# A graph-attention start-up put in a new order: exponentials shifted by an early maximum, a bound for the scale, three PSUM sets, and copies of Wh by ScalarE alone

## The chip, the cores and the metric

One NeuronCore of one Trainium2 chip runs the whole program. The metric is device time in microseconds. The engines are TensorE (PE, with its weight loads PEld), VectorE (DVE), ScalarE (ACT), GpSimd (POOL) and SyncE (SP); each runs its own instructions in the order in which the kernel writes them and waits for the others through semaphores.

## The reference, cut to what matters

```
Wh = x @ W                                       # x is 8192 x 128, W is 128 x 128
e  = leaky_relu((Wh @ a1)[:, None] + (Wh @ a2)[None, :], 0.2)   # s_i + t_j
e  = where(adj > 0, e, -9e15)                    # adj is 8192 x 8192 int32, sparse
x  = layernorm(x + elu(softmax(e, axis=1) @ Wh))
x1 = (adj @ x) / deg
x  = layernorm(x + concat([x1, x]) @ weight + bias)
```

## The kernel before

With s = Wh @ a1 and t = Wh @ a2, the exponential of leaky_relu(s_i + t_j) is a product of a factor of row i and a factor of column j, with one pair of factors where s_i + t_j is positive and another pair where it is negative. So the kernel makes, for each of the 64 tiles of 128 columns j, `factors`: Wh times e_j = exp(t_j - c) and Wh times f_j = exp(0.2 (t_j - c)), each as a high and a low float16 part, scaled by `scale_e` = 2^14 / max|Wh|, plus a denominator column for each part and a column of ones. The shift c is the largest t of all 8192. The main work of the first layer is then a matmul of 0/1 masks (edges that are positive, edges that are negative) with these factors (L679). Rows go in 32 groups of 256; a group takes 64 column tiles in eight `h` of 8 tiles, and an `h` is 4 x 8 matmuls (two row tiles times positive and negative). PE also packs the adjacency bits into 16-bit words (`pack_bits`, L640, for the first pair of groups, `pack_tile` in between matmuls, L628, later), ACT copies the words out of PSUM (`copy_words`, L422), and makes the level masks (`first_scores` L436 for the first group, `scores` L466 later). DVE unpacks words (L936, L938) and splits them into negative and positive masks (L1013, L1020). The second layer (L758, L819) follows after about 1000 us; the change does not touch it.

The change touches only the start, up to the end of the first group. There, in this order:

- SP loads x in nine pieces into the space of `factors[:, 1]`. PE turns W and makes W @ a (L594, L597), then for 16 blocks k of four tiles turns x (`turn_x`, L608) and multiplies by W and W @ a (`make_wh`, L617). A block goes to one of two pairs of PSUM banks. For each block ACT copies the turned x (`copy_turned`, L416), DVE copies s and t out of PSUM (`copy_s_t`, L865, semaphore wh_ok), and then ACT copies Wh out (`copy_wh`, L428, which waits for wh_ok). DVE also takes the largest |Wh| of each block (L871).
- After the last block DVE takes the largest and the smallest t, POOL makes them largest over the partitions (L366), ACT takes the exponentials e and f of all 64 tiles at once (L457, L458), and POOL reduces the largest |Wh| (L368).
- POOL issues the adjacency loads (L358), four of the first pair of groups after the sixth x piece, then those of the second pair, one after each `pack_bits`. Two `pack_bits` stand ahead of the first matmuls on PE.
- Then for each quarter c of the columns (16 tiles) DVE multiplies Wh by e and by f (`make_product` L923), ACT makes the high parts (`high_of` L504), and DVE the low parts (`low_of` L1028, `low_half` L1037 in the last quarter), unpacks and splits masks, and PE multiplies.

A product space has three slots. Each engine's order is written out by hand, so one engine that waits holds back all that stands behind it on that engine. What a group 1 matmul needs first is its masks (two ScalarE scores of 8 tiles for a quarter, an unpack, two splits) and the sums of group 0 taken off PSUM (L1051).

Of the kernel before, what the change touches and what calls it, by code (L numbers as in the profile page):

```python
# [32 lines left out]
P = 128  # L33
# [17 lines left out]
WIDEST = 10.0  # L51
# [7 lines left out]
def adj_resnorm_kernel(nc, x, adj, w0, a0, w1, b1, consts, out):  # L59
# [21 lines left out]
    with ctx:  # L81
# [3 lines left out]
        def sem(name):  # L85
# [11 lines left out]
        cols = sb("cols", [P, 12, NJ], F32)  # L97
# [9 lines left out]
        wh_top = sb("wh_top", [P, NX], F32)  # L107
# [6 lines left out]
        s_col, t_col, t_big, e_col, f_col, u_col, v_col, y_col, uy_col, vy_col, e_den, f_den = \  # L114
            (cols[:, k, :] for k in range(12))
        t_max, _, wh_max, wh_one, neg_t, neg_ft, inv_wh, scale_e, ones, sum_x = (one[:, k:k + 1] for k in range(10))
        t_max, t_spread = top_low[:, 2:3], wide_one[:, 7:8]
# [9 lines left out]
        wh = words[:, NG // 2:, :].rearrange("p g w -> p (g w)").bitcast(F32)[:, 0:NJ * F]\  # L127
            .rearrange("p (j f) -> p j f", f=F)
        early = words[:, 2:NG // 2, :].rearrange("p g w -> p (g w)").bitcast(F32)
        sizes, at, early_of = dict(product=3 * UNIT * F, wq=F + 2, w_turn=P, a_sb=2,  # L130
# [4 lines left out]
        product = early_of["product"].rearrange("p (k j f) -> p k j f", k=3, f=F)  # L135
        x_in = factors[:, 1, :, :].rearrange("p j r -> p (j r)").bitcast(F32)[:, 0:NJ * F]\
            .rearrange("p (k j f) -> p k j f", k=NX, f=F)
        x_t = product[:, 2, 0:2 * XB, :].rearrange("p (k j) f -> p k (j f)", k=2)
# [18 lines left out]
        pack_ps = [ctx.enter_context(nc.psum_tensor(f"pack_ps{k}", [P, 512], F32)) for k in range(2)]  # L157
# [16 lines left out]
        x_turned, x_t_ok, wh_made, wh_ok, top_ok = (sem(n) for n in "x_turned x_t_ok wh_made wh_ok top_ok".split())  # L174
        s_turned, s_turn_ok, sum_x_ok, sum_xb_ok = (sem(n) for n in "s_turned s_turn_ok sum_x_ok sum_xb_ok".split())
        mean_made, mean_ok, one_row_ok = (sem(n) for n in "mean_made mean_ok one_row_ok".split())
        t_top_ok, t_max_ok, wh_one_ok, wh_max_ok = (sem(n) for n in "t_top_ok t_max_ok wh_one_ok wh_max_ok".split())
        neg_ok, y_ok_col, uy_ok, exp_cols_ok, t_big_ok = (sem(n) for n in "neg_ok y_col_ok uy_ok exp_cols_ok t_big_ok".split())
        guard_ok, inv_ok, scale_ok, den_ok, den_hi_ok = (sem(n) for n in "guard_ok inv_ok scale_ok den_ok den_hi_ok".split())
# [55 lines left out]
        def wh_banks(k):  # L235
            return acc_banks[:, 2 * (k % 2):2 * (k % 2) + 2, 0:2 * (F + 2)].rearrange("p h (j f) -> p h j f", j=2)
# [115 lines left out]
        def _(pool):  # L352
# [7 lines left out]
            pool.memset(minus_half, -0.5).then_inc(half_ok, 1)  # L360
            pool.wait_ge(x_in_sem[NX // 2 - 3], 16)
            for c in range(UPG):
                load_adj(0, c, first=True)
            pool.wait_ge(t_top_ok, 1)
            pool.wait_ge(low_ok, 2)
            pool.partition_all_reduce(top_low[:, 2:4], top_low[:, 0:2], P, bass.bass_isa.ReduceOp.max).then_inc(t_max_ok, 1)  # L366
            pool.wait_ge(wh_one_ok, 1)
            pool.partition_all_reduce(wh_max, wh_one, P, bass.bass_isa.ReduceOp.max).then_inc(wh_max_ok, 1)  # L368

# [32 lines left out]
        def _(act):  # L402
# [3 lines left out]
            act.wait_ge(w0_turned, 1)  # L406
            act.activation(w_turn, turn_ps[0][:, 0:P], ACT.Copy).then_inc(w_turn_ok, 1)
            act.wait_ge(wa_made, 1)
            act.activation(wq[:, F:F + 2], turn_ps[1][:, 0:2], ACT.Copy).then_inc(wa_ok, 1)

# [14 lines left out]
            def copy_wh(k):  # L425

                act.wait_ge(wh_ok, k + 1)
                act.activation(wh[:, XB * k:XB * (k + 1), :].rearrange("p (h j) f -> p h j f", h=2),  # L428
                               wh_banks(k)[:, :, :, 0:F], ACT.Copy).then_inc(wh_copied, 1)
# [11 lines left out]
            for k in range(NX):  # L441
# [5 lines left out]
                if k:  # L447
                    copy_wh(k - 1)
            copy_wh(NX - 1)
            act.wait_ge(s_row_ok, 1)  # L450
            act.wait_ge(s_turned, 1)
            act.activation(s_turn, turn_ps[0][:, 0:P], ACT.Copy).then_inc(s_turn_ok, 1)
            first_scores(0, 2)


            act.wait_ge(neg_ok, 2)
# [24 lines left out]
            def group(g, slot, loads, next_words, before_last=None, second=False):  # L481
# [3 lines left out]
                for h in range(8):  # L485
                    if h or not second:
                        scores(g, slot, h)
                    if second and h == UPG + 1:
                        act.wait_ge(wh_saved, 1)
                        act.wait_ge(e_low_ok, UPG + 1)  # L490
                        act.wait_ge(f_low_ok, UPG + 1)
# [863 lines left out]
```

## Time and profile before

| | |
|---|---|
| median of three runs | 1486.92 us (1486.07 to 1487.76) |
| profiled execution, its span | 1484.3 us |
| what lies around the span | about 2.6 us (median less span) |
| PE busy in the span | 1449.9 us (98%) |
| DVE, ACT, POOL busy | 994.9, 936.4, 118.3 us |
| granted TensorE clock, mean | 0.991 |

The span runs from the first to the last instruction of one profiled execution. "Idle before" in a row of the timeline is the time in which the engine had nothing to do just ahead of that row, and the arrow says what ended it. In timeline rows several instructions of one kind are merged: the count stands behind the x and the length is that of all together. An instruction's length overlaps the start of the next one by about 0.1 us on DVE and ACT, so the text reckons from start to start.

### The profile page before, as it was taken

To read this page: it belongs to the slowest core of one execution; us is meant where nothing else is said; L and a number is where in the kernel's file an instruction comes from. 1 tells how busy PE (TensorE), PEld (TensorE's weight loads), DVE (VectorE), ACT (ScalarE), POOL (GpSimd) and SP (SyncE) were. 2 spreads that over 40 slices of the span, in tenths; PEclk is the share of its full clock that TensorE was granted. 3 is DMA by queue.
4 is the path that set the end of the run, shared out by engine and by line. 5 is a ranking of instruction groups with operands and counts; after the bars stand their busy time and mean duration, and the time that the engine had idled before them with its cause. 6 is when DMAs were issued, how large, how long until landed. Compare 5 with 4: busy or idle time off the path is not lost.

```text
span 1484.3 us, 33988 instructions
## 1 busy us (share of the span) xinstructions
PE 1449.9 (98%) x12110; PEld 1107.8 (75%) x12110; DVE 994.9 (67%) x2833; ACT 936.4 (63%) x2289; POOL 118.3 (8%) x199
## 2 busy tenths in 40 slices
PE   7599999999999999999999999999999999999998
PEld 7578888888888888888888888884454545454557
DVE  4998888888788888878887887773433343334332
ACT  6989999999999999999999999940000000000000
POOL 1001000100010010001000100000000000000000
PEclk9799999999999999999999999999999999999999
DMA  9969997788788868877886882041000000000000
GB/s 174 111 71 101 120 108 90 83 94 95 84 86 96 93 78 95 94 90 82 95 94 83 87 96 37 19 119 49 22 15 21 14 21 14 21 14 21 14 15 15
DMA packets 99201, 101.47 MB, mean 68 GB/s; under 512 B 4432, under 2 KB 66384, under 8 KB 99152
## 3 DMA queue, kind: packets, MB, share of 16 engines
q0 software_dynamic: 33792, 67.11, 45.5%
q1 hardware_dynamic: 64800, 33.57, 8.7%
q8 instruction: 31, 0.51, 0.1%
q10 hardware_dynamic: 560, 0.14, 0.1%
q14 instruction: 18, 0.15, 0.0%
HBM read 289.48 MB, written 12.65 MB: 204 GB/s over the span
## 4 chain that ended last, share of the span: by engine, by line
PE 90%; DMA 2%; DVE 1%; issue 0%; POOL 0%; ACT 0%; SPq 0%; DVEq 0%; POOLq 0%
PE acc L679 58%; PE pack_ps L758 27%; PE pack_ps L819 2%; DMA adj_space<-in_adj 2%; PE acc L793 1%; PE pack_ps L628 1%; PE turn_ps L780 1%; PE turn_ps L769 0%; DMA level_ring<-x_rows 0%; DMA x_parts<-parts 0%; POOL one L378 0%; DVE adj_space L945 0%; DVE stats L1118 0%; DVE part_sums L1051 0%; DVE edge_ring L1020 0%
## 5 line engine op out<-in xcount | busy, mean ns | idle before, releaser
L466 ACT ACTIVATE level_ring<-s_row,cols 128x256 fp8e4<-128x256 f32 x1984 | 803.7, 495 | 0.0
L679 PE MATMUL acc<-factors,edge_ring 128*128 128x259 f16 x4096 | 548.8, 274 | 14.5 <-DVE edge_ring L1020 13.0
L679 PE MATMUL acc<-factors,level_ring 128*128 128x259 f16 x4096 | 548.3, 274 | 0.0
L758 PE MATMUL pack_ps<-adj_space,factors 128*128 128x512 fp8e4 x1920 | 421.7, 379 | 0.9 <-issue 0.9
L679 PEld LDWEIGHTS acc<-factors,edge_ring 128*128 128x128 fp8e4 x4096 | 365.9, 98 | 64.8 <-issue 15.8
L679 PEld LDWEIGHTS acc<-factors,level_ring 128*128 128x128 fp8e4 x4096 | 366.5, 98 | 48.9
L758 PEld LDWEIGHTS pack_ps<-adj_space,factors 128*128 128x128 f16 x1920 | 187.9, 98 | 217.6 <-issue 1.1
L1013 DVE TENSOR_TENSOR level_ring<-level_ring,edge_ring 128x1024 uint16<-128x1024 uint16 x256 | 171.2, 689 | 103.7 <-ACT level_ring L466 93.3
L1190 DVE TENSOR_SCALAR adj_space<-words 128x512 uint16 (+1 forms) x448 | 96.3, 288 | 146.7 <-PE pack_ps L758 146.6
L628 PE MATMUL pack_ps<-pack_w,adj_space 128*128 128x32 bf16 x960 | 170.7, 178 | 0.0
L1020 DVE TENSOR_TENSOR edge_ring<-edge_ring,level_ring 128x1024 uint16<-128x1024 uint16 x256 | 166.7, 683 | 0.1
L558 ACT ACTIVATE level_ring<-turn_ps 128x512 f32<-128x512 f32 x16 | 9.6, 597 | 217.4 <-PE turn_ps L769 217.4
L566 ACT ACTIVATE level_ring<-pack_ps 128x256 f32<-128x256 f32 x30 | 9.9, 381 | 212.6 <-PE pack_ps L758 212.6
L936 DVE TENSOR_SCALAR edge_ring<-words 128x512 uint16 (+1 forms) x448 | 106.1, 297 | 8.6 <-issue 6.4
L376 POOL TENSOR_SCALAR one<-mv 128x2 f32<-128x2 f32 x64 | 18.9, 295 | 1075.1 <-DVE mv L1125 1075.1
L628 PEld LDWEIGHTS pack_ps<-pack_w,adj_space 128*128 128x128 fp8e4 x960 | 91.6, 95 | 14.1
L1219 DVE SCALAR_TENSOR_TENSOR level_ring<-acc,cols,level_ring 128x128 f32<-128x128 f32 x64 | 19.4, 346 | 96.8 <-PE acc L793 96.8
L945 DVE SCALAR_TENSOR_TENSOR adj_space<-adj_space 128x1024 int32<-128x1024 int32 x60 | 73.1, 1218 | 0.9 <-DMA adj_space<-in_adj 0.9
L358 POOL DMA_DIRECT2D adj_space<-in_adj x64 | 51.3, 802 | 260.5 <-PE pack_ps L628 195.8
L422 ACT ACTIVATE words<-pack_ps 128x512 f32 (+1 forms) x64 | 38.1, 595 | 39.7 <-PE pack_ps L628 39.7
L378 POOL TENSOR_TENSOR one<-one 128x2 f32<-128x2 f32 x64 | 48.0, 750 | 9.5
L1130 DVE TENSOR_SCALAR level_ring<-level_ring,mv,one 128x128 f32<-128x128 f32 x64 | 19.3, 344 | 41.5 <-POOL one L378 41.5
(104 smaller groups left out, 726.8 us busy)
## 6 DMA issues: line engine op xcount, KB each, us to landing
adj_space<-in_adj POOLq DMA_DIRECT2D x64, 1024.0 KB, 14.5
rows_x<-in_x SPq DMA_DIRECT2D x32, 128.0 KB, 2.1
x_rows<-rows_y SPq DMA_DIRECT2D x32, 128.0 KB, 9.7
x_parts<-parts SPq DMA_DIRECT2D x32, 128.0 KB, 4.4
factors<-x_parts SPq DMA_DIRECT2D x8, 512.0 KB, 4.8
level_ring<-x_rows SPq DMA_DIRECT2D x16, 256.0 KB, 2.8
out<-level_ring SPq DMA_DIRECT2D x32, 128.0 KB, 1.8
s_row<-s_and_t SPq DMA_DIRECT2D x30, 128.0 KB, 3.0
```

The lines of the kernel that those rows point to most:

```text
L358: pool.dma_start(adj_ring[:, c, :, :], adj_tiles[n, :, :, c * COLS:(c + 1) * COLS]).then_inc(adj_in[c], 16)
L378: pool.tensor_tensor(rstd, var_eps, minus_half, ALU.pow).then_inc(rstd_sem, TPG)
L422: act.activation(row_words[:, n, c * WPU:(c + 1) * WPU], pack_ps[c % 2][:, 0:WPU], ACT.Copy)\
L466: a = act.activation(level_bytes[:, h % MASK_SLOTS, j, :], s_row[:, slot, :], ACT.Relu, bias=t_big[:, h * HALF + j:h * HALF + j + 1], scal ...
L628: return pe.matmul(pack_ps[c % 2][:, j * WPR:(j + 1) * WPR], nibbles, pack_w[:, 0, :], start=True, stop=True)
L679: m = pe.matmul(acc[a][:, 0:WIDE_ROW], mask, factors[:, neg, jj, 0:WIDE_ROW], start=(jj == 0), stop=(jj == NJ - 1))
L758: m = pe.matmul(pack_ps[slot][:, :], factors[:, 0, jj, part * F:(part + 1) * F], ring_1_bytes[:, c, j, :], start=(jj == 0 and part == 0), ...
L936: d = dve.tensor_scalar(to, src, 6 - k, EDGES, ALU.logical_shift_left, ALU.bitwise_and)
L945: dve.scalar_tensor_tensor(out=pair[:, 0], in0=pair[:, 1], scalar=1, in1=pair[:, 0], op0=ALU.logical_shift_left, op1=ALU.bitwise_or).then_ ...
L1013: dve.tensor_tensor(level, level, edge_ring[:, c % EDGE_SLOTS, k * HALF:(k + 1) * HALF, :], ALU.bitwise_and).then_inc(neg_ready, 1)
L1020: dve.tensor_tensor(edges, edges, level_ring[:, (2 * c + k) % MASK_SLOTS, :, :], ALU.bitwise_xor)\
L1190: d = dve.tensor_scalar(to, src, 6 - k, EDGES, ALU.logical_shift_left, ALU.bitwise_and)
```

## The change

- `base`, the largest t of the first 16 tiles (over all partitions), replaces the largest t of all as shift c. `t_exp` is t bounded from above by base + 1. e and f are made in four quarters (`exponentials(c)`) and no longer at once. The test for a wide spread of t is adapted (`WIDEST` 7.5, `RISE` 1).
- `wh_one`, from which the scale comes, is no longer the largest |Wh| but the product of the largest |x| (`top_of_x`, nine reductions) and the largest absolute column sum of W.
- ACT copies Wh and the two columns s and t in one instruction (`copy_wh`, now 130 columns a tile), and DVE's copies (L865) and maxima (L871) go. The s column of that space is then overwritten with `wh_one`, so product, high part and low part have 129 columns and make the denominators too; the six DVE instructions for denominators (L956, L962, L971) go.
- `make_wh` uses three PSUM sets (two of `acc`, one of `pack_ps`). W is turned after x's first block.
- Inside the loop of 16 blocks ACT now also makes 8 `first_scores` (k = 6 to 13), two quarters of exponentials (k = 8, 11) and `high_of(0)` (k = 14).
- POOL takes `base` over the partitions ahead of the adjacency loads, and takes over y, uy and vy from DVE.
- PE does `pack_bits(0)` and `(1)`, then turns s and t, and goes to the masks' matmuls. DVE and ACT have a new order by hand in the first group.

```diff
-            for k in range(NX):
+            copy_turned(0)
+            act.wait_ge(w0_turned, 1)
+            act.activation(w_turn, pack_ps[0][:, 0:P], ACT.Copy).then_inc(w_turn_ok, 1)
+            copy_turned(1)
+            act.wait_ge(wa_made, 1)
+            act.activation(wq[:, F:F + 2], pack_ps[0][:, P:P + 2], ACT.Copy).then_inc(wa_ok, 1)
+            copy_wh(0)
+            for k in range(2, NX):
                 copy_turned(k)
...
-                if k:
-                    copy_wh(k - 1)
+                copy_wh(k - 1)
+                if 6 <= k < 14:
+                    first_scores(k - 6, k - 5)
+                if k == 8:
+                    exponentials(0)
+                if k == 11:
+                    exponentials(1)
+                if k == 14:
+                    high_of(0)
             copy_wh(NX - 1)
...
+            exponentials(2)
+            high_of(1)
+            first_scores(8, 12)
+            copy_words(0, 0)
+            exponentials(3)
+            first_scores(12, 16)
+            high_of(2)
+            first_scores(16, 20)
+            copy_words(0, 1)
             act.wait_ge(s_turned, 1)
             act.activation(s_turn, turn_ps[0][:, 0:P], ACT.Copy).then_inc(s_turn_ok, 1)
...
+            high_of(3)
+            first_scores(20, 32)
+            high_of(4)
+            high_of(5)
+            first_scores(32, 40)
+            copy_words(0, 2)
+            first_scores(40, 48)
+            high_of(6)
+            high_of(7)
+            copy_words(0, 3)
+            first_scores(48, 64)
+            act.wait_ge(uy_ok, 2)
+            act.activation(u_col, uy_col, ACT.Exp).then_inc(exp_cols_ok, 1)
+            act.activation(v_col, vy_col, ACT.Exp).then_inc(exp_cols_ok, 1)
...
+            def first_unpack(c):
+                dve.wait_ge(mask_used, 2 * c + 2)
+                dve.wait_ge(words_ok, c + 1)
+                unpack(0, 0, c, edge_ring, c).then_inc(unpacked, 1)
+            def split(c, k):
+                negative(0, c, k)
+                positive(0, c, k)
...
+            top_column(0)
+            make_product(0)
+            scaled_t(2)
+            bounded_t(2)
+            top_column(1)
+            make_product(1)
+            low_of(0, e_low_ok)
+            dve.wait_ge(wh_copied, NX)
...
+            top_column(2)
+            top_column(3)
+            make_product(2)
+            first_unpack(0)
+            split(0, 0)
+            dve.wait_ge(x_turned, NX)
+            dve.memset(factors[:, 1, :, ROW:WIDE_ROW], 1.0).then_inc(edge_col_ok, 1)
+            low_of(1, f_low_ok)
+            split(0, 1)
+            make_product(3)
+            low_of(2, e_low_ok)
...
+            first_unpack(1)
+            split(1, 0)
+            low_of(3, f_low_ok)
+            split(1, 1)
+            make_product(4)
+            make_product(5)
+            low_of(4, e_low_ok)
+            first_unpack(2)
+            split(2, 0)
+            low_of(5, f_low_ok)
+            split(2, 1)
+            make_product(6)
+            make_product(7)
+            sum_of_x()
+            low_of(6, e_low_ok)
+            first_unpack(3)
+            low_of(7, f_low_ok)
+            split(3, 0)
+            split(3, 1)
```

## Rows read from the trace of the kernel before

**Rows 1.** The page, part 4: lines on the chain that ended last.

```profile
PE acc L679 58%; PE pack_ps L758 27%; PE pack_ps L819 2%; DMA adj_space<-in_adj 2%; PE acc L793 1%; PE pack_ps L628 1%; PE turn_ps L780 1%; PE turn_ps L769 0%; DMA level_ring<-x_rows 0%; DMA x_parts<-parts 0%; POOL one L378 0%; DVE adj_space L945 0%; DVE stats L1118 0%; DVE part_sums L1051 0%; DVE edge_ring L1020 0%
```

**Rows 2.** Busy time by stretch: PE, PEld, DVE, ACT, POOL, PEclk, DMA share, GB/s.

```profile
40.00:50.00 10.00, 1.89 (x44) 1.49 (x39) 9.81 (x23) 10.00 (x20) 0.74 (x1) 0.50 1.07 115
200.00:400.00 200.00, 200.00 (x1975) 176.44 (x1974) 164.09 (x424) 188.33 (x468) 19.43 (x28) 1.00 0.81 92
```

**Rows 3.** Timeline of PE: start us, length us, line, work, count, idle before.

```profile
7.14 0.56 PE L597 MATMUL turn_ps<-words 128*128 128x2 f32 x2 [1.62 <-DMA words<-in_a]
...
9.85 2.10 PE L617 MATMUL acc<-words 128*128 128x130 f32 x8
...
21.00 0.60 PE L608 MATMUL turn_ps<-consts_sb,factors 128*128 128x128 f32 x4
21.43 1.06 PE L617 MATMUL acc<-words 128*128 128x130 f32 x8
...
39.23 1.87 PE L640 MATMUL pack_ps<-pack_w,adj_space 128*128 128x32 bf16 x64 [3.92 <-issue]
...
50.12 1.89 PE L679 MATMUL acc<-factors,edge_ring 128*128 128x259 f16 x8 [7.28 <-DVE edge_ring L1020]
...
93.21 1.05 PE L679 MATMUL acc<-factors,edge_ring 128*128 128x259 f16 x8 [0.54 <-DVE part_sums L1051]
```

**Rows 4.** Timeline of ACT, the same columns.

```profile
16.80 0.19 ACT L416 ACTIVATION_READ_ACCUMULATOR words<-turn_ps 128x1 f32 x1
16.89 0.59 ACT L445 ACTIVATE s_row<-pack_ps 128x512 f32<-128x512 f32 x1
...
33.36 0.60 ACT L428 ACTIVATE words<-acc 128x512 f32<-128x512 f32 x1 [0.70 <-DVE cols L865]
...
35.19 0.35 ACT L457 ACTIVATE cols<-cols,one 128x64 f32<-128x64 f32 x1 [0.27 <-DVE one L897]
...
38.87 0.58 ACT L422 ACTIVATE words<-pack_ps 128x512 uint16<-128x512 f32 x1
39.35 3.89 ACT L504 ACTIVATE factors<-words,one 128x2048 f16<-128x2048 f32 x2
...
43.61 8.09 ACT L436 ACTIVATE level_ring<-s_row,cols 128x256 fp8e4<-128x256 f32 x20
```

**Rows 5.** Timeline of DVE, the same columns.

```profile
34.95 0.14 DVE L896 TENSOR_SCALAR one<-top_low 128x1 f32<-128x1 f32 x1
...
47.05 0.90 DVE L936 TENSOR_SCALAR edge_ring<-words 128x512 uint16<-128x512 uint16 x4
...
50.39 4.49 DVE L923 TENSOR_TENSOR words<-words,cols 128x2048 f32<-128x2048 f32 x2
54.80 4.61 DVE L1028 SCALAR_TENSOR_TENSOR factors<-words,one,factors 128x2048 f16<-128x2048 f32 x2
...
83.68 0.68 DVE L1013 TENSOR_TENSOR level_ring<-level_ring,edge_ring 128x1024 uint16<-128x1024 uint16 x1
84.40 0.69 DVE L1020 TENSOR_TENSOR edge_ring<-edge_ring,level_ring 128x1024 uint16<-128x1024 uint16 x1
```

**Rows 6.** Timeline of POOL, the same columns.

```profile
14.43 3.18 POOL L358 DMA_DIRECT2D adj_space<-in_adj  x4 [13.46 <-DMA factors<-in_x]
34.01 0.38 POOL L366 PARTITION_ALL_REDUCE top_low<-top_low  x1 [16.40 <-DVE top_low L890]
...
71.71 0.74 POOL L358 DMA_DIRECT2D adj_space<-in_adj  x1 [9.81 <-PE pack_ps L640]
```

**Rows 7.** Issue to landing of the adjacency load issued at 14.43 us.

```profile
DMA to landing us min/median/max: 14.3/14.3/14.3
```

**Rows 8.** Issue to landing of the adjacency load issued at 71.71 us.

```profile
DMA to landing us min/median/max: 26.8/26.8/26.8
```

**Rows 9.** Issue to landing of the adjacency load issued at 115.73 us.

```profile
DMA to landing us min/median/max: 13.0/13.0/13.0
```

**Rows 10.** Issue to landing of the second x load, issued at 1.39 us.

```profile
factors<-in_x SPq DMA_DIRECT2D x1, 512.0 KB, 5.4
```

More of the change, by code:

```diff
@@ L113, in adj_resnorm_kernel @@
         ident = consts_sb[:, 0:P]
[L114 to L117, printed above, removed]
+        s_col, t_col, t_big, e_col, f_col, u_col, v_col, y_col, uy_col, vy_col, t_exp = \
+            (cols[:, k, :] for k in range(11))
+        x_most, w_most, _, wh_one, neg_t, neg_ft, inv_wh, scale_e, ones, sum_x = (one[:, k:k + 1] for k in range(10))
+        x_most, w_most = tops[:, 2:3], tops[:, 3:4]
+        base_top, base, base_rise = tops[:, 4:5], tops[:, 5:6], tops[:, 6:7]
+        t_max, t_spread, t_rise = top_low[:, 2:3], wide_one[:, 7:8], tops[:, 7:8]
         half_max, row_max, neg_max, half_sum, row_sum = (wide_one[:, a:b] for a, b in ((0, 2), (2, 3), (3, 4), (4, 6), (6, 7)))
@@ L613, in make_wh @@
                 pe.wait_ge(x_t_ok, k + 1)
-                if k >= 2:
-                    pe.wait_ge(wh_copied, k - 1)
+                if k == 6:
+                    pe.wait_ge(s_row_ok, 1)
+                elif set_of[k] in set_of[0:k]:
+                    last = max(i for i in range(k) if set_of[i] == set_of[k])
+                    pe.wait_ge(wh_copied, last + 1)
                 for j in range(XB):
@@ L652, in _ @@
             turn_x(0)
+            pe.wait_ge(w0_in, 16)
+            pe.transpose(pack_ps[0][:, 0:P], wq[:, 0:F], ident).then_inc(w0_turned, 1)
+            turn_x(1)
+            pe.wait_ge(w_turn_ok, 1)
+            pe.wait_ge(a0_in, 16)
+            pe.matmul(pack_ps[0][:, P:P + 2], w_turn, a_sb, start=True, stop=True).then_inc(wa_made, 1)
+            pe.wait_ge(wa_ok, 1)
             for k in range(NX):
-                if k + 1 < NX:
+                if 0 < k < NX - 1:
                     turn_x(k + 1)
@@ L696, in group @@
                         multiply(g, h, pack_chunk=pack_chunk)
-            pe.wait_ge(wh_copied, NX)
-            pack_bits(1)
-            wide = is_wide(pe)
-            pe.wait_ge(sum_xb_ok, 1)
-            pe.matmul(turn_ps[1][:, 0:F], sum_xb, wq[:, 0:F], start=True, stop=True).then_inc(mean_made, 1)
-            pe.wait_ge(den_hi_ok, 4)
-            pe.wait_ge(edge_col_ok, 1)
             for c in range(UPG):
                 for h in (2 * c, 2 * c + 1):
-                    multiply(0, h, c == UPG - 1 or h % 2 == 0, True)
+                    multiply(0, h, h % 2 == 0, True)
                 if c < 2:
                     pack_bits(c + 2)
+                if c == 1:
+                    wide = is_wide(pe)
+                if c == 2:
+                    pe.wait_ge(sum_xb_ok, 1)
+                    pe.matmul(turn_ps[1][:, 0:F], sum_xb, wq[:, 0:F], start=True, stop=True).then_inc(mean_made, 1)
             group(1, {1: (1, 0), 2: (1, 1), 3: (1, 2)})
```

298 lines of the change are left out of this document (135 added, 163 removed).

## The prediction

> **What bounds the kernel now.** I read the chain that ended last first: PE's own matmuls hold it [rows 1]. The table of stretches then shows where PE is not full: from 200 us on it is busy all the time at full clock, and in the start it is busy 1.89 of 10 us between 40 and 50 us, at half clock, while VectorE and ScalarE are full [rows 2]. So the end moves by as much as the first matmul of group 1 moves (93.21 us [rows 3]), if nothing later catches up or falls behind. ScalarE is busy 188.33 of 200 us in the steady part [rows 2], so what is late there comes back slowly, and PE, which is the bound, never gives it back. Last I read the timelines of the start for each operation's price.
>
> **Prices, start to start.** ScalarE: a copy of 512 columns 0.49 us, the accumulator read 0.09, words 0.48, a high part 1.90 (two in 3.89), a score 0.40 (20 in 8.09), an exponential of 64 columns 0.25 and of 16, by estimate, 0.15 [rows 4]. VectorE: product 2.20 (two in 4.49), low part 2.27, unpack until its first use 0.95, negative and positive mask of one h 0.72 and 0.61, so a `split` 1.33, small ones 0.08 [rows 5]. A full 129-column product, high or low part is 0.01 longer. PE: `turn_x` 0.43, `make_wh` 0.90; cold, `make_wh` 1.9 [rows 3]. A semaphore adds about 0.05, an estimate from the gap between a length's end and the next engine's start. With the order of the kernel before, these prices and waits put group 1 at 93.0, against 93.21 measured, so they carry a sum over engines.
>
> **The head.** The second x load lands at 1.39 + 5.4 = 6.8 [rows 10]. W @ a now stands behind `turn_x(1)`, not ahead of both turns; with cold turns it ends near 8.3, `make_wh(0)` starts near 8.9 and not at 9.85 [rows 3]. That 0.95 is mostly lost again in the first blocks, which alternate PE and ScalarE: I reach the accumulator read of block 4 at 16.7 (16.80 before [rows 4]).
>
> **The loop.** What is removed, VectorE's copy between `make_wh` and `copy_wh` and its reductions of Wh, is a wait that hardly counted: PE's 0.43 + 0.90 = 1.33 us a block [rows 3] was the pace, and ScalarE's 0.49 + 0.09 + 0.49 = 1.07 fitted in. The third PSUM set removes a wait behind which PE was full anyway. What is added counts: with one score a block ScalarE needs 1.48, and becomes the pace. After the read at 16.7 ScalarE has 0.09, s_row 0.52, copy_wh(3) 0.50, eleven blocks of 1.08 (11.9), 8 scores (3.2), 4 exponentials (0.6), high_of(0) (1.9) and the last copy (0.5), in all 19.2, and waits 1.1, of which 0.8 for `make_wh(15)`, which high_of(0) has held back. So it leaves the loop at 37.0; before it did at 33.36 + 0.49 = 33.85 [rows 4]. The loop ends **3.1 us later**, with 8 scores (3.2), all but two of the exponentials and one high part (1.9) done ahead.
>
> VectorE's nine reductions of x (1.1 each by the product's rate of 2048 elements in 2.2) follow the loads, and lie beside the loop. The scale is ready near 26.8, the first product at 29.5, three us before high_of(0) at 32.7 wants it. POOL's reduction over partitions isn't longer than 0.94: 34.01 to the consumer's 34.95, which shows no wait [rows 5, 6]; up to 3 us more would stay covered there.
>
> **Adjacency.** The loads now wait for `base`, so they are issued at 19.0 and not at 14.43 [rows 6]. A lone load lands after 13.0 [rows 9]; queued ones follow each 10 us (the first landed 14.3 after its issue at 14.43, at 28.7, and the eighth at 71.71 + 26.8 = 98.5 [rows 6 to 8]: (98.5 - 28.7) / 7). New landings: 32.0, 41.9, 51.8, 61.8, then to 101.5. `pack_bits(1)` can't start before 41.95 (39.23 before [rows 3]), and now stands ahead of every masks' matmul: the first matmul is at 43.9 instead of 50.12 [rows 3]. Words of the second quarter are used only at 52, so these 2.7 us are covered. Joins of the second pair move later with group 1 and keep 15 us of margin.
>
> **After the loop**, the likeliest course, link by link:
> - ScalarE from 37.0: two exponentials, high(1), four scores, words(0): 4.4. VectorE, idle 1.0, unpacks at 41.4.
> - VectorE: unpack 0.95, split, low(1), split, product(3), low(2), 0.4 of small ones, unpack 1.25 (0.3 of it a wait for a score), split, low(3), split, product(4) 2.35: 19.2. ScalarE is done with scores 20 to 31 at 56.4 and **waits 4.2** for product(4), after 2.4 for product(3). It gets it at 60.65.
> - ScalarE: high(4), 0.3 wait, high(5), eight scores, words(2): 8.0. VectorE **waits 3.6** for words(2), until 68.6; the score that the next split wants comes no earlier.
> - VectorE: unpack, split, low(5), split, product(6): 8.2, to 76.8. ScalarE **waits 5.2**.
> - ScalarE: high(6), 0.3, high(7), words(3), 16 scores (6.4), u and v (0.3), 16 scores of group 1 (6.4): 17.8, to 94.6. VectorE waits 1.9, 1.1 and 2.6 for scores.
> - VectorE: mask operations 1.8, the scaling of group 0's sums 0.55: 2.4. Group 1 starts at **97.1**.
>
> 37.0 + 4.4 + 19.2 + 8.0 + 8.2 + 17.8 + 2.4 = 97.0. The work of both engines alone would have allowed less: the two of them hand over in turn, with 11.8 us of ScalarE waiting for products. PE starts 6.2 us earlier than before and loses it in waits of 0.7, 5.9 and 4.7 for masks; the cold clock that follows them falls in time it does not need. What VectorE is spared (denominators, about 1.5, and y, uy and vy, 0.3) is on no wait of this chain.
>
> Against the profile (my 93.0 for 93.21) this is +4.1 us: span 1488.4, median 1486.92 + 4.1 = **1491.0**.
>
> **A rule of the Trainium skill.** The POOL rows show no lock: four load issues took 3.18 us beside VectorE's work, 0.8 each [rows 6]. "SBUF — State Buffer", section "SBUF: two separate sides", says that GpSimd and VectorE share a port pair as an exclusive lock, and that a DMA issued by GpSimd can starve for its descriptors. By it, POOL's loads, and y, uy and vy which it now computes, could be late beside VectorE's two-input products; the trace can't show the lock itself.
>
> **Rivals.**
> - *The waits overlap, faster.* If VectorE gets to product(4) 4 us earlier than I sum, ScalarE does not stop, and the later waits shrink. Bound: VectorE's own list from 37.2 (six products 13.3, seven low parts 16.0, four unpacks 3.8, eight splits 10.6, group 1's masks and sums 4.0, rest 2.2) ends at 87.1, so group 1 at 87.1, -6.1 us: 1480.8. It decides from 4 us less waiting on. For it: both engines have the work done ahead. Against: each handover is in the written order. 12%.
> - *The loop costs less, no change.* A clock that rises at 10 us and waits of 0.03 for 0.05 give group 1 near 95.3, +2.3: 1489.2. 24%, with all that ends within 0.2%.
> - *As summed, or up to 2 us more.* Cold turns until 15 us give 98.4, +5.4. 52%.
> - *Adjacency late, by the port or the queue.* Landings 6 us later put group 1 at 97.9 and from there each us costs one; 9 us give +8: 1495. By the rule above this is where it would show. 12%.
> - *The exact path.* If the test for wide t fired, 64 slow tiles would follow. From the reference's inputs the largest t is 1.46, the first 16 tiles' 1.14, the smallest -1.49: both tests are under 7.5. 0%.
>
> **Numbers.** Changes of 0.2% (3.0 us) are about what a measurement of this kernel can tell. Slower by more: 0.62 (most of the summed case and the late adjacency). Within: 0.25. Faster: 0.13. The likeliest case's own range is 1489.2 to 1493.0. The range takes in the cheap loop and the late adjacency, and a part of an overlap: 1485.0 to 1495.0.
>
> **What would show it.** Right: ScalarE's last `copy_wh` at 36 to 37; first masks' matmul at 43 to 45; ScalarE idle some 4 us ahead of the fifth high part and 5 ahead of the seventh; VectorE idle 3 to 4 ahead of the third unpack; group 1 at 96 to 98.5; later stages shifted by the same amount. Wrong: no idle at these handovers, or PE waiting for `pack_bits(1)` past 45, or a later stage which moves by another amount than group 1.

## The result, and the profile after

The changed kernel takes **1490.70 us** (median of 14 runs, 1489.70 to 1491.41) against 1487.24 us (14 runs, 1486.07 to 1488.27) for the kernel before: ratio 1.0022, 95% interval [1.0015, 1.0029]. That is slower by 3.5 us; the forecast was 1491.0, slower by 4.1. In the profiled executions the span went from 1484.3 to 1488.8 us, by 4.5, at the same mean TensorE clock (0.991 and 0.992). The profiled execution of the changed kernel took 1490.74 us, as its median, 1.9 more than its span. Where the kernel before has its time and its span on record for the same execution (58 of them, beside the experiments), the time is 1.7 to 1.8 us longer, and not the 2.6 that the table ahead of the prediction has by setting a median against the span of another execution. By estimate, then, the profiled execution of before took 1486.05 us, 1.2 below its median. That makes the 4.5 us of the spans and the 3.5 of the medians one finding.

The table of stretches for the kernel before, from the end of the loop to the start of group 1 (columns: stretch, its length, busy us of PE, PEld, DVE, ACT, POOL with their counts, granted clock, DMA share, GB/s):

```profile
37.00:99.00 62.00, 45.22 (x503) 37.76 (x504) 60.44 (x91) 61.08 (x124) 2.23 (x3) 0.81 1.04 109
```

The same stretch, and the steady one of [rows 2], for the changed kernel:

```profile
37.00:99.00 62.00, 42.69 (x518) 34.82 (x515) 51.70 (x76) 49.74 (x100) 7.43 (x8) 0.83 1.06 111
200.00:400.00 200.00, 200.00 (x1975) 176.43 (x1972) 162.52 (x415) 188.45 (x467) 19.14 (x28) 1.00 0.82 92
```

Read these first. In the start both VectorE and ScalarE had been full (60.44 and 61.08 of 62 us); now each is idle for 10 to 12 us of it, and still group 1 starts later. That is not less work. A fixed stretch counts only what falls into it: VectorE now does 3.9 us more ahead of 37 us (19.77 for 15.90) and ScalarE 1.5 (25.66 for 24.14), and what waits pushed behind 99 us is not counted. Up to its first matmul of group 1 each kernel keeps VectorE busy for the same time, 70.72 us before and 70.73 now. ScalarE has 79.43 and 74.65, but before it had made 36 scores of group 1 by then and now 23, which is about those 5 us. VectorE's copies and maxima (L865 and L871, 13.5 us) are gone, but nine reductions of x (9.8 us) and other small ones came in their place. What the change brought is work done earlier and idle time behind it. From 200 us on PE is full as it was in [rows 2], so what the start loses stays lost.

The timeline of PE, changed kernel (columns as in [rows 3]):

```profile
8.54 2.10 PE L648 MATMUL acc<-words,edge_ring 128*128 128x130 f32 x8 [0.35 <-ACT words L477]
...
13.88 1.21 PE L648 MATMUL acc<-words,edge_ring 128*128 128x130 f32 x8
...
42.24 1.89 PE L671 MATMUL pack_ps<-pack_w,adj_space 128*128 128x32 bf16 x64 [3.75 <-DMA adj_space<-in_adj]
...
44.67 1.89 PE L720 MATMUL acc<-factors,edge_ring 128*128 128x259 f16 x8 [0.25 <-DVE factors L1195]
...
72.31 1.89 PE L720 MATMUL acc<-factors,edge_ring 128*128 128x259 f16 x8 [6.13 <-DVE edge_ring L1001]
...
87.61 1.89 PE L720 MATMUL acc<-factors,edge_ring 128*128 128x259 f16 x8 [6.01 <-DVE edge_ring L1001]
...
98.26 1.05 PE L720 MATMUL acc<-factors,edge_ring 128*128 128x259 f16 x8 [0.93 <-DVE part_sums L1023]
```

The masks' matmuls start 5.45 us earlier than in [rows 3] (44.67 for 50.12), and group 1 starts 5.05 us later (98.26 for 93.21). Between the two, PE stands idle for 6.1 us ahead of the third quarter's masks and for 6.0 ahead of the fourth's. A stage later 0.4 of the 5.05 came back: group 2's first matmul is at 158.09 with 0.51 us of idle ahead of it, where before it was at 153.41 with 0.88; the rest of the span moved as group 2 did, within 0.2 us.

The timeline of ACT, changed kernel:

```profile
36.94 0.60 ACT L441 ACTIVATE words<-acc 128x520 f32<-128x520 f32 x1 [0.76 <-PE acc L648]
...
50.38 2.04 ACT L469 ACTIVATE factors<-words,one 128x2064 f16<-128x2064 f32 x1 [2.31 <-DVE words L938]
...
61.66 2.04 ACT L469 ACTIVATE factors<-words,one 128x2064 f16<-128x2064 f32 x1 [4.46 <-DVE words L938]
...
77.88 2.03 ACT L469 ACTIVATE factors<-words,one 128x2064 f16<-128x2064 f32 x1 [5.12 <-DVE words L938]
```

The timeline of DVE, changed kernel:

```profile
42.02 0.90 DVE L951 TENSOR_SCALAR edge_ring<-words 128x512 uint16<-128x512 uint16 x4 [0.89 <-ACT words L435]
...
69.67 0.90 DVE L951 TENSOR_SCALAR edge_ring<-words 128x512 uint16<-128x512 uint16 x4 [3.55 <-ACT words L435]
...
89.08 0.69 DVE L994 TENSOR_TENSOR level_ring<-level_ring,edge_ring 128x1024 uint16<-128x1024 uint16 x1 [1.77 <-ACT level_ring L449]
...
92.56 0.69 DVE L994 TENSOR_TENSOR level_ring<-level_ring,edge_ring 128x1024 uint16<-128x1024 uint16 x1 [0.81 <-ACT level_ring L527]
...
95.75 0.69 DVE L994 TENSOR_TENSOR level_ring<-level_ring,edge_ring 128x1024 uint16<-128x1024 uint16 x1 [2.50 <-ACT level_ring L527]
```

ScalarE waits for VectorE's products (L938) at 50, 62 and 78 us, VectorE waits for ScalarE's words (L435) at 42 and 70 and for scores from 89 on. Each wait ends when the other engine has come out of its own. The chain that ended last between 38 and 98 us shows the same in order, with start and length of each piece (pieces under 0.1 us are left out):

```profile
59.32 4.53 DVE words L938 x2
63.87 2.03 ACT factors L469
65.91 2.02 ACT level_ring L449 x6
67.93 0.26 issue
68.19 0.89 ACT level_ring L449 x2
69.08 0.49 ACT words L435
69.67 0.16 DVE edge_ring L951
...
75.54 4.53 DVE words L938 x2
80.09 2.04 ACT factors L469
82.13 0.47 ACT words L435
82.60 2.43 ACT level_ring L449 x7
```

After 42 us it crosses between the two engines four times, and among the pieces that the view lists none is of PE, POOL or a DMA.

### The profile page after: what moved, and what is told of

Its sections match the earlier page's. It is cut to its first block, busy times and chain, and to the rows that moved or that the text cites. A ratio compares the mean times of both kernels' runs of the same rounds, so it can differ in the third digit from the quotient of the medians.

```text
span 1488.8 us, 34001 instructions
## 1 busy us (share of the span) xinstructions
PE 1453.4 (98%) x12110; PEld 1109.4 (75%) x12110; DVE 994.3 (67%) x2816; ACT 937.0 (63%) x2295; POOL 121.0 (8%) x203
## 4 chain that ended last, share of the span: by engine, by line
PE 92%; ACT 3%; DMA 2%; DVE 2%; issue 1%; POOL 0%; DVEq 0%; SPq 0%; POOLq 0%; ACTq 0%
PE acc L720 58%; PE pack_ps L797 28%; PE pack_ps L858 2%; DMA adj_space<-in_adj 2%; PE acc L832 1%; PE pack_ps L659 1%; PE turn_ps L819 1%; ACT level_ring L449 1%; DVE words L938 1%; PE acc L648 1%; PE turn_ps L808 0%; ACT factors L469 0%; ACT level_ring L527 0%; DMA factors<-in_x 0%; DVE factors L1009 0%
## 5 line engine op out<-in xcount | busy, mean ns | idle before, releaser
L720 PE MATMUL acc<-factors,edge_ring 128*128 128x259 f16 x4096 | 549.6, 275 | 14.4 <-DVE edge_ring L1001 12.7
L435 ACT ACTIVATE words<-pack_ps 128x512 f32 (+1 forms) x64 | 38.0, 594 | 39.3 <-PE pack_ps L659 39.3
L1102 DVE TENSOR_SCALAR level_ring<-level_ring,mv,one 128x128 f32<-128x128 f32 x64 | 19.3, 344 | 41.5 <-POOL one L396 41.5
```

The costliest lines, as they stand in the source:

```text
L435: act.activation(row_words[:, n, c * WPU:(c + 1) * WPU], pack_ps[c % 2][:, 0:WPU], ACT.Copy)\
L720: m = pe.matmul(acc[a][:, 0:WIDE_ROW], mask, factors[:, neg, jj, 0:WIDE_ROW], start=(jj == 0), stop=(jj == NJ - 1))
```

## The experiments

Each ran beside the kernel before on the same chip; that kernel's medians there were 1487.32, 1487.37 and 1487.23 us. Diffs are against the changed kernel unless said otherwise. "Group 1" is the start of its first matmul, 98.26 us in the changed kernel. Of 12 kernels I begin with those that undo one part each.

**1. Two PSUM sets.**

```diff
-        set_of = [0, 1, 0, 1, 0, 1, 2, 0, 1, 2, 0, 1, 2, 0, 1, 0]
+        set_of = [k % 2 for k in range(NX)]
```

> The changed kernel with two PSUM sets in place of three. If the third set buys nothing (the copies of Wh and of turned x on ScalarE are the pace of the loop, and PE is full before that): group 1 starts at 98.3 as in the changed kernel, within 0.3, time 1490.7 within 1. If the third set hides a wait in the loop, the loop of 16 blocks gets up to 0.4 us longer in each of the ten blocks from k = 6 on, up to 4 us in all: 1491.5 to 1494.7.

Measured: 1490.86 us, 1.0021 [1.0012, 1.0031]. The loop ended with a copy at 36.93 (36.94) and group 1 began at 98.28. The third set is worth nothing: PE's queue is never held by a set in this loop.

**2. The adjacency loads later**, behind POOL's second reduction.

```diff
             pool.partition_all_reduce(base, base_top, P, bass.bass_isa.ReduceOp.max).then_inc(base_ok, 1)
+            pool.wait_ge(x_top_ok, NX // 2 + 3)
+            pool.partition_all_reduce(tops[:, 2:4], tops[:, 0:2], P, bass.bass_isa.ReduceOp.max).then_inc(x_w_ok, 1)
             pool.wait_ge(x_in_sem[NX // 2 - 3], 16)
...
-            pool.wait_ge(x_top_ok, NX // 2 + 3)
-            pool.partition_all_reduce(tops[:, 2:4], tops[:, 0:2], P, bass.bass_isa.ReduceOp.max).then_inc(x_w_ok, 1)
```

> The changed kernel with the first four adjacency loads behind POOL's second reduction, issued at 26.4 and not at 18.96. Handover theory: pack_bits(1) and the first masks' matmul come 7 us later (near 49.5 and 52), of which the wait for product(3) and VectorE's list behind it swallow 5: group 1 at 100.4, +2.2, time 1492.9. Adjacency theory: all 7 us go through, 1497.7.

Measured: 1492.68 us, 1.0038 [1.0023, 1.0052]; issue at 25.40 for 18.96. The timeline of PE with the late loads:

```profile
49.31 1.89 PE L671 MATMUL pack_ps<-pack_w,adj_space 128*128 128x32 bf16 x64 [8.80 <-DMA adj_space<-in_adj]
```

The second pack moved by 7.07 us (49.31 for 42.24) and group 1 by 1.23 (99.49). The loop of this execution had ended 0.84 us earlier (last copy at 36.10 for 36.94; the last section shows where that comes from), so the late loads cost 2.1, and by the medians 2.0. Some 5 of the 7 us are covered, and the loads of the changed kernel are not what it pays for.

**3. The adjacency loads first**, ahead of POOL's reduction of `base`, issued at 14.34 as in [rows 6].

```diff
-            pool.wait_ge(base_top_ok, 1)
-            pool.partition_all_reduce(base, base_top, P, bass.bass_isa.ReduceOp.max).then_inc(base_ok, 1)
             pool.wait_ge(x_in_sem[NX // 2 - 3], 16)
...
+            pool.wait_ge(base_top_ok, 1)
+            pool.partition_all_reduce(base, base_top, P, bass.bass_isa.ReduceOp.max).then_inc(base_ok, 1)
```

> The changed kernel with the adjacency loads issued as before, at 14.4, ahead of the reduction of base. Handover theory: pack_bits(1) near 39.5, group 1 unmoved at 98.3, time 1490.7. Adjacency theory: 2.7 us are won back, 1488.0.

Measured: 1495.58 us, 1.0055 [1.0038, 1.0072], 4.9 us worse than the changed kernel. No theory had this. The timeline of POOL:

```profile
14.34 3.19 POOL L369 DMA_DIRECT2D adj_space<-in_adj  x4 [13.37 <-DMA factors<-in_x]
25.83 0.38 POOL L376 PARTITION_ALL_REDUCE tops<-tops  x1 [8.30 <-issue]
30.03 0.37 POOL L378 PARTITION_ALL_REDUCE tops<-tops  x1 [3.83 <-DVE tops L1167]
```

The issues end at 17.53, and the reduction that needs 0.38 us starts 8.30 us later, which the view puts down to "issue". Its operand is ready at 18.0 (VectorE's L1154, 17.83 us), so some 7.8 us of it are no wait that the trace shows. ScalarE's exponentials inside the loop then wait 3.29 us for `base`, the loop's last copy is at 41.74 instead of 36.94, and group 1 at 103.08: 4.8 later each. Two explanations stood: four DMA issues leave work behind on POOL that delays its next instruction, or POOL's first partition reduction of the program costs 8 us whenever it comes, and in the changed kernel it is hidden in a wait of 17.7 us.

**4. The same with a reduction at POOL's very start**, whose result nothing reads (diff against experiment 3).

```diff
+            pool.wait_ge(half_ok, 1)
+            pool.partition_all_reduce(one[:, 22:24], minus_half, P, bass.bass_isa.ReduceOp.max).then_inc(primed, 1)
```

> adj_first (loads issued at 14.4, ahead of the reduction of base) with one more reduction over partitions on POOL at its very start, whose result nothing reads. In adj_first POOL stood idle 8.3 us between the fourth load issue and the reduction of base, all that it waited for being long there. If POOL makes ready for its first reduction in that time: primed, the reduction of base runs at 18, pack_bits(1) near 39.5, group 1 at 97.5 to 98.3, time 1490 to 1490.7, which is also what shows an early load worth nothing. If POOL is busy after the issues themselves (writing descriptors): the gap of 8.3 us and 1495.6 stay.

Measured: 1490.66 us, 1.0024 [1.0014, 1.0034]. The timeline of POOL:

```profile
11.00 0.37 POOL L374 PARTITION_ALL_REDUCE one<-one  x1 [10.02 <-issue]
14.66 3.32 POOL L370 DMA_DIRECT2D adj_space<-in_adj  x4 [3.29 <-DMA factors<-in_x]
19.01 0.37 POOL L379 PARTITION_ALL_REDUCE tops<-tops  x1 [1.03 <-DVE tops L1157]
```

The idle moved with the first reduction: 10.02 us ahead of it, with no DMA issued by POOL yet, and none ahead of the one that follows the four issues. The descriptors are out as the cause. Now that loads are early and `base` is in time, `pack_bits(1)` no longer waits, but the timeline of PE shows the first masks' matmul no earlier:

```profile
45.02 1.89 PE L723 MATMUL acc<-factors,edge_ring 128*128 128x259 f16 x8 [4.43 <-DVE factors L1198]
```

L1198 is the `memset` of the column of ones, which stands behind the first `split` in VectorE's list. So this matmul waits for VectorE's first masks and that `memset`, and the early load is worth nothing. In the changed kernel the same `memset` (there L1195) ended PE's wait of 0.25 us at 44.67, with `pack_bits(1)` already done. The forecast of the changed kernel's adjacency term, nothing, holds in both directions.

**5. y, uy and vy on VectorE again**, behind the test for wide t.

```diff
-            pool.wait_ge(base_ok, 1)
-            pool.wait_ge(cols_ok, UPG)
-            pool.tensor_tensor(y_col, s_col, base.to_broadcast([P, NJ]), ALU.add).then_inc(y_ok_col, 1)
...
+            dve.wait_ge(base_ok, 1)
+            dve.wait_ge(cols_ok, UPG)
+            dve.tensor_tensor(y_col, s_col, base.to_broadcast([P, NJ]), ALU.add).then_inc(y_ok_col, 1)
...
```

> The changed kernel with y, uy and vy on VectorE again (behind the test for wide t), and not on POOL, where they stood idle 10.7 us ahead of the first of them and delayed the load of the second pair from 39 to 53. Handover theory: that load is issued at 39, VectorE's 0.3 us lies in its idle time, group 1 at 98.3 to 98.6, time 1490.7 to 1491. If POOL's delay is on the path: up to 14 us of landing time, seen as less than 1489.

Measured: 1490.99 us, 1.0030 [1.0019, 1.0042]; loop and group 1 both 0.8 to 0.9 earlier than in the changed kernel's trace, so nothing between them changed. POOL's next load was issued at 38.31 instead of 53.32, without any gain. The 0.8 us did not reach the end: group 2 starts 0.5 earlier (157.57), but the span is 1489.0, 0.2 longer. What took them back isn't known. Within that, who computes y does not count.

**6. A busy PE in the head**: eight transposes whose results nothing reads, three ahead of each `turn_x` and two ahead of `make_wh(0)`.

```diff
+            for _ in range(3):
+                pe.transpose(pack_ps[1][:, 0:P], ident, ident)
             turn_x(0)
...
```

> The changed kernel with eight added transposes of the unit matrix on PE in the head, three ahead of turn_x(0), three ahead of turn_x(1), two ahead of the wait for W @ a, whose results nothing reads. In the changed kernel make_wh still took 1.73 us a block at 11.3 and the loop ended 0.4 later than I had summed with a clock that rose at 12.3. If cold matmuls in the head are that term: make_wh(0) or (1) takes 0.9, the loop's end and group 1 move 1.5 to 3 us earlier (group 1 at 95.5 to 97), time 1488.0 to 1489.3. If they aren't: 1490.7, or up to 0.5 more for the added matmuls.

Measured: 1489.91 us, 1.0014 [1.0005, 1.0024]; group 1 at 97.25. The timeline of PE:

```profile
11.28 1.72 PE L648 MATMUL acc<-words,edge_ring 128*128 128x130 f32 x8
12.84 0.60 PE L636 MATMUL turn_ps<-consts_sb,factors 128*128 128x128 f32 x4
```

`turn_x(2)` already runs at the fast rate (0.60), where in the changed kernel the `make_wh` at 13.88 is the first near it. But the executions of experiments 2 and 5 had this `turn_x` just as fast without any filler, so the trace doesn't show that the filler did it. The interval of the ratio overlaps with that of the changed kernel: inconclusive, with 0.8 us by the medians. One thing stays open: 4 of the 10 executions took 1488.13 to 1488.92 us, and none of the changed kernel's 14 was under 1489.70. The profiled execution (1489.65) was not one of the four, so no trace shows what they did.

**7. The loop kept lean**: no scores and no high part in it, all of that right behind it.

```diff
-                if 6 <= k < 14:
-                    first_scores(k - 6, k - 5)
...
-                if k == 14:
-                    high_of(0)
             copy_wh(NX - 1)
+            high_of(0)
             exponentials(2)
             high_of(1)
-            first_scores(8, 12)
+            first_scores(0, 12)
             copy_words(0, 0)
```

> The changed kernel with the eight scores and high_of(0) taken out of the loop and put right behind it, ScalarE's order otherwise kept. Handover theory: the loop ends near 33.2, 3.7 us earlier, but that work now lies ahead of high_of(1), so group 1 starts 1.4 later, at 99.6, time 1492.1. Loop theory (the 3.1 us by which the loop ends later are the loss): 3.1 us are won, 1487.6.

Measured: 1492.46 us, 1.0035 [1.0022, 1.0049]. The loop's last copy came at 33.22, 3.7 us earlier, and group 1 at 99.67, 1.4 later. That the filled loop is by itself the loss is refuted: its 3 us are paid for work that has to be done anyway.

**8. Only the words and eight scores ahead of two high parts** on ScalarE.

```diff
-            first_scores(20, 32)
+            first_scores(20, 40)
+            copy_words(0, 2)
             high_of(4)
             high_of(5)
-            first_scores(32, 40)
-            copy_words(0, 2)
```

> The changed kernel; on ScalarE alone the scores 32 to 39 and copy_words(0, 2) stand ahead of high_of(4) and high_of(5), and not behind them. Handover theory: they fill the 4.5 us in which ScalarE waited for product(4), VectorE no longer waits 3.55 for words(2), group 1 starts 3.6 earlier at 94.6, time 1487.1. Adjacency or cold-clock theory (first masks' matmul held by pack_bits(1), then PE slow): nothing moves, 98.3 and 1490.7.

Measured: 1487.08 us, 0.9998 [0.9989, 1.0007], 3.6 us better than the changed kernel; group 1 at 94.42. The timeline of ACT:

```profile
61.45 2.04 ACT L469 ACTIVATE factors<-words,one 128x2064 f16<-128x2064 f32 x1 [0.51 <-DVE words L937]
...
74.03 2.03 ACT L469 ACTIVATE factors<-words,one 128x2064 f16<-128x2064 f32 x1 [5.15 <-DVE words L937]
```

The wait of 4.46 us became 0.51, VectorE no longer waits for the third words (3.55 before), and group 1 came 3.84 us earlier. Moving two calls takes back what the whole change lost.

**9. ScalarE's order anew**, nothing else.

```diff
...
-            first_scores(20, 32)
+            first_scores(24, 44)
             high_of(4)
-            high_of(5)
-            first_scores(32, 40)
             copy_words(0, 2)
-            first_scores(40, 48)
+            high_of(5)
+            first_scores(44, 52)
             high_of(6)
-            high_of(7)
             copy_words(0, 3)
-            first_scores(48, 64)
+            high_of(7)
+            first_scores(52, 64)
...
```

> The changed kernel with a new order on ScalarE alone after the loop (words as soon as packed, scores ahead of the high parts that wait for products, last 12 scores behind high_of(7)). Handover theory: 6.2 us less than the changed kernel, group 1 at 92.0, time 1484.5, since VectorE's own order still leaves about 5.6 us of waits. If the handovers cost nothing: 1490.7.

Measured: 1484.01 us, 0.9978 [0.9969, 0.9988]; group 1 at 92.08. ScalarE's waits for products fell to 0.80 and 4.98 us.

**10. ScalarE's and VectorE's orders anew**: products ahead of the splits and low parts that do not need them. VectorE's part of the diff, its core:

```diff
             first_unpack(0)
+            make_product(3)
             split(0, 0)
...
-            make_product(3)
             low_of(2, e_low_ok)
+            first_unpack(1)
+            make_product(4)
+            make_product(5)
+            low_of(3, f_low_ok)
+            split(1, 0)
...
```

> The changed kernel with a new order on ScalarE and on VectorE after the loop (products made earlier, ahead of the masks that wait for scores). Handover theory: 9.8 us less than the changed kernel, group 1 at 88.4, VectorE idle under 3 us between 38 and 88, time 1480.9, 6 less than before. Loop theory (the 3.1 us of a later loop end are lost whatever stands behind): group 1 not under 93.2 + 3.1 = 96.3, time 1489 or more. Adjacency theory: 1490.7.

Measured: 1481.86 us, 0.9964 [0.9951, 0.9978]; group 1 at 89.49, with 256 matmuls of L722 ahead of it as in the other kernels. The timeline of PE:

```profile
73.42 1.05 PE L722 MATMUL acc<-factors,edge_ring 128*128 128x259 f16 x8 [3.71 <-DVE edge_ring L1003]
...
75.93 1.94 PE L722 MATMUL acc<-factors,edge_ring 128*128 128x259 f16 x8
...
89.49 1.05 PE L722 MATMUL acc<-factors,edge_ring 128*128 128x259 f16 x8
```

No row between 73.42 and 89.49 shows PE waiting. So the handovers have ended by then, and what is left is PE's own queue, with two blocks of matmuls at 1.84 and 1.94 us where 1.05 is usual. ScalarE waits for a product for 0.7 us in all (12.3 in the changed kernel), and VectorE is busy 48.78 of the 50 us from 38 on. This makes it 8.8 us less than the changed kernel by group 1 and by the medians, for 9.8 expected.

**11. Both orders and a lean loop**: orders on both engines found anew, so they differ from those of 10, with no scores in the loop and `high_of(0)` one block earlier (k = 13).

> New orders on ScalarE and VectorE as in both_orders, found anew with no scores in the loop and high_of(0) one block earlier (k = 13): group 1 at 86.3 to 86.9, 1 to 1.5 us earlier than both_orders (87.72), time 1480.6; ScalarE without idle time between 38 and 85. If VectorE's own list is already the floor in both_orders: no change against it, 1481.9.

Measured: **1478.93 us**, 0.9946 [0.9932, 0.9959]; group 1 at 86.11. The 87.72 in this expectation is a misreading of experiment 10, two blocks of 8 matmuls too early; against 89.49 the gain is 3.4 us. The table of stretches shows both engines full again, here until group 1:

```profile
37.00:86.00 49.00, 38.28 (x451) 32.23 (x451) 47.70 (x62) 49.00 (x104) 9.53 (x7) 0.86 1.06 111
```

Its view of waits between 33 and 98 us (engine and line, what it waited for, us in total, times, longest):

```profile
...
DVE top_low L1185 <- ACT words L441: 1.1, 1, 1.1
DVE level_ring L996 <- ACT level_ring L529: 0.7, 1, 0.7
```

ScalarE waits for no product at all, and VectorE 1.8 us in 65; in the changed kernel the same view of the same stretch has 12.3 and 11.5 us:

```profile
...
ACT factors L469 <- DVE words L938: 12.3, 5, 5.1
...
DVE edge_ring L951 <- ACT words L435: 4.4, 2, 3.6
DVE level_ring L994 <- ACT level_ring L527: 3.3, 2, 2.5
DVE factors L1009 <- ACT factors L469: 2.0, 1, 2.0
...
DVE level_ring L994 <- ACT level_ring L449: 1.8, 1, 1.8
```

**12. The same with the busy head of 6.**

> lean_both with the eight added transposes of warm_head, where the loop ran 0.7 us earlier. If that gain is kept through an order without slack: 0.7 less than lean_both, time 1479.9, 7 us less than the kernel before.

Measured: 1478.56 us, 0.9938 [0.9924, 0.9952], span 1476.5 against 1476.6. By the medians there is no difference from 11 that could be told. But again 2 of 5 executions (1477.06 and 1477.22) lie 1.4 us under the lowest of 11 (1478.59), and the profiled one isn't among them. The filler may help in some executions; what it does there stays open.

Over these kernels group 1 and the median move together: 98.26 and 1490.70, 94.42 and 1487.08, 92.08 and 1484.01, 89.49 and 1481.86, 86.11 and 1478.93. Group 1 moved by 12.2 us from the first to the last of them and the median by 11.8, and on the way the two stay within about 0.5 us of each other. VectorE's busy time up to group 1 stays where it was all the while (70.73 us in the changed kernel, 70.96 in experiment 10, 69.85 in 11). So the order took out waiting and not work.

## Why the prediction was right

**The course.** Link by link, forecast and measured (us):

| link | forecast | measured |
|---|---|---|
| ScalarE leaves the loop | 37.0 | 37.44 |
| VectorE gets words(0) | +4.4 | +4.58 |
| ScalarE gets product(4) | +19.2 | +19.64 |
| VectorE gets words(2) | +8.0 | +8.01 |
| ScalarE gets product(6) | +8.2 | +8.21 |
| the last score that VectorE waits for | +17.8 | +17.87 |
| group 1 | +2.4 (97.1) | +2.51 (98.26) |

The waits were forecast as 2.4, 4.2 and 5.2 for ScalarE and 3.6, 1.9, 1.1 and 2.6 for VectorE; they measured 2.31, 4.46 and 5.12, and 3.55, 1.77, 0.81 and 2.50. Only PE's last wait for masks was off, 4.7 forecast and 6.01 measured, without an effect on group 1. That these handovers, and not the work, set the end was a reading of the sum; experiments 8 to 11 show it, by taking group 1 12 us forward with little besides the order of the same instructions. The kernel before had no such waits to take out: from 37 us to its group 1 VectorE was idle for 1.4 us (54.82 busy of 56.21), so a new order alone could have given it little. That is argued from its trace; no run of it was made.

**The head.** The first `make_wh` was at 8.54 (8.9 forecast, 9.85 before) and the read of block 4 at 16.95 (16.7). PE's slow first matmuls took their share here: the prediction had their end at 10 us as the cheap case and at 15 as the dear one, and the sum lay between. The `make_wh` at 11.29 took 1.94 us and the one at 13.88 took 1.21, so the slow rate ended near 14. Where it ended one block earlier the loop ended 0.84 us sooner (experiment 2); the forecast missed its end by 0.44.

**Loop.** It ended 3.6 us later than before (37.44 for 33.85; 3.1 forecast), by ScalarE's added work. As a reason for the loss, "the loop ends later" would have been wrong: experiment 7 takes it away and loses 1.8 us more. The prediction's sum had that work done ahead on its other side, and so did not fall for it.

**Adjacency.** `pack_bits(1)` at 42.24 (41.95 forecast), the first masks' matmul at 44.67 (43.9), both covered. The rival that loads come late by a port or a queue is out: four issues took 3.32 us (3.18 in [rows 6]), and the first load landed 12.7 us after its issue (13.0 forecast). Its price was right: 6 us later was to cost 0.8 and each further one 1.0, so 7.07 us 1.9; experiment 2 measured 2.0 to 2.1.

**The third PSUM set** was put at nothing and is (experiment 1). **POOL's y** was put on no wait. It came at 49.34, 10 us later than its operands allow, but uy and vy are wanted at 89, so nothing paid for it (experiment 5). Part of what the prediction said of two-input products is seen here and cost nothing: uy took 2.38 us for vy's 0.49 (the last section has the rows).

**The size.** That the time came out within 0.3 us of 1491.0 is partly luck, since misses cancelled. Against the profiled execution group 1 was to move by 4.1 us from the reckoned 93.0, and moved by 5.05 from 93.21. Of the 1.2 us by which 97.1 was too early, 0.44 are the loop, 0.44 the link to product(4) and 0.18 the link to words(0); the other links were right within 0.11. (The prices of the link to product(4), as the prediction lists them, add up to 19.3 and not 19.2.) The span moved by 0.4 more than forecast, as part of the 5.05 came back by group 2. On the other side the 4.1 was added to the median of the kernel before, though it was reckoned from the trace of an execution that took 0.9 us less than that median by the estimate above.

**The faster rival** needed VectorE to reach product(4) 4 us earlier. The lists of both engines nearly allow it (87.1 was its bound; experiment 10 came to 89.5 and experiment 11, with a lean loop, to 86.1), but not in the order as written. Its 6.1 us were reckoned from 93.21 where the other cases go from 93.0; on that basis they are 5.9, and 1481.0. So the change made room for a gain, and its hand-written order spent it on waits.

## What to carry to other kernels

Where two engines hand over to each other in turn in an order written by hand, add up each engine's list in that order with its waits, not its busy time: between 37 and 99 us both were busy for some 10 us less here, and the end came later. A busy time that falls in a fixed stretch can be work that was done earlier or is still to come, so compare it up to the same point of the program. Put independent work (scores here) between the instruction that asks for the other engine's result and the last thing that engine needs from this one, and give each engine what the other waits for first. Before work is moved into a loop, or an extra buffer is counted as a gain, ask whether the chain behind it has to do that work anyway, and whether the engine ever waited for a buffer.

## What the hardware showed unexpectedly

**POOL's first call of a kind.** The first partition reduction on POOL costs 8 to 10 us of its own, shown as "issue": 8.30 us in experiment 3 (7.8 behind its operand), 10.02 at POOL's start in experiment 4, and none ahead of the reductions that follow. In the changed kernel it lies inside a wait of 17.7 us and can't be seen. The first two-input operation behind the reductions pays again. The timeline of POOL, changed kernel:

```profile
38.26 0.37 POOL L381 PARTITION_ALL_REDUCE top_low<-top_low  x1 [11.89 <-DVE top_low L1186]
49.34 1.15 POOL L384 TENSOR_TENSOR cols<-cols,tops 128x64 f32<-128x64 f32 x1 [10.71 <-issue]
50.59 2.38 POOL L386 TENSOR_SCALAR cols<-cols 128x64 f32<-128x64 f32 x1
```

It was 10.1 to 12.7 us in each kernel where POOL makes y. That code is loaded at these places is a guess. The queue named "instruction" moved one to three packets in some of them, but it moved some in other stretches too, and none at all in the 10.02 us at the start of experiment 4. So the cause stays open. The Trainium skill, "GPSIMD Engine Reference", section "2.1 Instruction dispatch", says that the first call to a freshly loaded kernel also pays a load of about 6 us that no instruction in the profile shows. Whether these waits are that load no run here shows; they are longer, 7.8 to 12.7 us. An engine that looks free can thus be 10 us late with its first operation of a kind; a call whose result nothing reads, placed in an idle stretch, paid it ahead in experiment 4.

**A POOL operation held up by VectorE's two-input ones.** Each of POOL's three operations for y, uy and vy took 0.46 to 0.59 us where it was short. The 2.38 us of the row at 50.59 end at 52.97, 0.3 us behind this one of VectorE:

```profile
50.26 2.40 DVE L1009 SCALAR_TENSOR_TENSOR factors<-words,one,factors 128x2064 f16<-128x2064 f32 x1
```

The same holds in all 12 kernels in which POOL makes y. The first of the three, of 0.58 to 2.32 us, always ends 0.15 or 0.16 us behind a product or a low part of VectorE, and each of the others that took over 0.6 us ends 0.3 to 0.4 us behind one. In experiment 11 two in a row took 2.38 and 2.29 us beside two products. So in these traces a two-input operation of VectorE holds up such an operation of POOL until it has ended, as the prediction took it could. That one causes the other is read from these coincident ends; no run takes the two apart. POOL's load issues show nothing of the kind, with 0.8 us each.

**PE's slow start ends at a different moment in each execution.** The changed kernel and experiments 2, 5, 8, 9 and 10 have the same instructions on PE in the head and the loop. The second `make_wh` of the loop took 1.94 us at 11.29 in the changed kernel, but less, with a fast `turn_x(2)` behind it, in experiment 5. The timeline of PE there:

```profile
11.45 1.41 PE L642 MATMUL acc<-words,edge_ring 128*128 128x130 f32 x8
12.70 0.60 PE L630 MATMUL turn_ps<-consts_sb,factors 128*128 128x128 f32 x4
```

The step from 1.94 to 1.06 us for the same block is about that between stretches with a granted clock of 0.50 and of 1.00 (1.89 us for 8 masks' matmuls at 44.67, 1.05 at 49.37). But the granted clock of the profile reads 1.00 for every us from 8 to 16 in both executions, so in the head the two rates are read from the lengths alone. The slow rate ended between 12 and 15 us, in one execution earlier than in another, and the end of the same loop moved with it between 36.07 and 37.58 us (last copy; experiment 5 the first, 9 the last, the changed kernel 36.94). In experiment 9 `make_wh(0)` itself was 0.44 us later, behind the load of a. A single profile of this kernel can't be used to tell 0.8 us in the start.
